# A four-step 16-bit minimum for the key distances, and a quarter of the dense units masked through ScalarE and TensorE

## The chip, the cores and the metric

One core of a Trainium2 chip runs the whole program. The metric is the device time of one execution in microseconds (us). Engines are named as in the profile: PE (TensorE matmul), PEld (its weight loads), DVE (VectorE), ACT (ScalarE), POOL (GpSimd), SP (SyncE, which only issues DMAs).

## The reference, cut to what matters

32 independent items (batches) go through three stages. A convolutional tokenizer makes 128 channels by 64 positions. A linear-attention mixer works on rows of 64. Then a product-key feed-forward with 8 heads follows, of which the core is:

```
sim = einsum(q, pk_keys)                  # two lists of 64 scores per row and head
scores, idx = top_k(sim, 16)              # the best 16 of each list
score = scores[0][:, None] + scores[1][None, :]      # 256 pairs
final_scores, pk_idx = top_k(score, 16)   # the best 16 pairs -> rows of a 4096-row table per head
weights = softmax(final_scores)
kv = sum over the 16 chosen rows of weights * table[row]
```

The table has 4096 rows per head, each of 128 numbers (64 of key, 64 of value); a small causal attention per head follows on kv.

## The kernel before, in words

Each batch is cut into stages: tokenizer (T), mixer (M), `route` (R, top 16 and row numbers of heads 0 to 3), `second` (S, the same for heads 4 to 7), `dense` (D), `group` (G, sums of gathered rows) and `head` (H, the attention).

Heads 0 to 4 are **gathered**: POOL issues 16 indirect DMAs per head (L1090), each fetching 128 rows of 512 bytes into one of three buffers `got`. These are 5 x 16 x 32 = 2560 gathers. A gather of group n waits for the PE sum of group n-3 (`s_summed`, L1381), because there are three buffers; group 0 of a batch waits for the row numbers that `route` writes (L1930), group 4 for those of `second` (L2127). PE sums a group at hop `a{g}`, which waits until the group has landed.

Heads 5 to 7 are **dense**: no rows are fetched, but all 4096 table rows of the head, kept in SBUF (`tab`, 2 MB a head, three heads), are multiplied by weights of which all but 16 are zero. A head has 16 units of 256 rows, a batch has 48, the kernel 1536. A unit u is: PE `p{u}` (`pair_scores`: two matmuls L1337 for the scores, two matmuls L1339 for the distances, 128x128 bf16 each, into one of two PSUM banks); ACT `x{u}` (L1642, exp of the 256 scores); DVE `w{u}` (L2203, which keeps the weight where the distance is under 15.5); PE `v{u}` (`table_sum`, L1359, two fp32 products, four records).

The **distance** of each of the 64 keys of a list from the chosen ones is made in `second`, hops `o{i}{k}`, for the 6 lists of the dense heads: four DVE additions give 64 x 16 differences in fp16 (L2150, 256 elements each), and two reductions over the last axis of 16 take the smallest absolute value (L2155, 512 elements in, 32 out each). Both lists' distances are added in the matmuls L1339.

The **order** of all work is written out by hand-made tables: `AT` gives every hop of every stage a due time in units of a millionth of a batch, `OWN` replaces it for some batches, `plan()` sorts all hops of all batches, and each engine issues its instructions in that one order. Nothing is chosen at run time: an engine waits at the front of its queue. Before the change the sorted order has, on DVE ahead of the first row numbers of batch 0, the hops `r0` to `row_d` of `second` and `n0` of batch 2's tokenizer.

Of the kernel before, what the change touches and what calls it, by code (L numbers as in the profile page):

```python
# [19 lines left out]
F16 = mybir.dt.float16  # L20
ALU = mybir.AluOpType
# [18 lines left out]
DENSE = (5, 6, 7)  # L40
ND = len(DENSE)
NG = HEADS - ND
# [3 lines left out]
UNITS = ND * TILES  # L46
# [16 lines left out]
QUARTER = 4  # L63
PARTS = 4
# [74 lines left out]
def tower(nc, x, consts, pairs, w0, w1, w2, w3, cvec, mw1, mw2, mw3, mb1, mb2, mb3, stack, mix, bw, ba, bg, vec64,  # L139
          wo_attn, gn, wqpk, keys, wq, table, wo_ffn, parts, out):  # L140
    ctx = ExitStack()
    with ctx:
# [135 lines left out]
        tab = sb("tab", [P, ND, CHUNKS, P])  # L278
        d_w = sb("d_w", [P, 2, 2, P])
        kvd = sb("kvd", [P, ND, P])  # L280
# [81 lines left out]
        s_stack = [sem(f"s_stack{i}") for i in range(2)]  # L362
        s_pairs = sem("s_pairs")
        s_d_exp = sem("s_d_exp")
        s_d_w = sem("s_d_w")
        s_d_sum = sem("s_d_sum")
# [30 lines left out]
        block = ctx.enter_context(nc.Block())  # L397

# [31 lines left out]
        for n, k in enumerate(("xd", "proj", "lora", "ss", "tri", "p0", "t0", "p1", "t1", "p2", "t2", "p3", "t3", "p4", "t4",  # L430
# [8 lines left out]
        R2 = {k: n for n, k in enumerate(each_list + [  # L439
            "idx", "cand", "keys", "fin8", "codes", "code", "rep_f0", "rep_f1", "rep_f2", "rep_f3", "fin16_0", "fin16_1", "fin16_2", "fin16_3", "fidx",  # L440
            "place", "early", "shift", "pick_e0", "row_e0", "pick_l0", "row_l0",
            "row_d", "row_t", "rep_d", "row_h", "code0", "chosen", "code1", "depth", "code2", "code3"]
            + [f"{k}{i}{j}" for i in range(ND) for j in range(2) for k in ("miss", "near", "half", "dist")]
            + ["fsum", "frec", "weight", "w_t", "shifted"], 1)}
        NROUTE, NSECOND = len(R), len(R2)

# [19 lines left out]
        def group_hops(u):  # L466

            last = u == UNITS - 1
            return ([(f"v{u - 1}", 0.9)] if u else []) + ([(f"k{u - 1}", 0.4)] if u and u % TILES == 0 else []) + (
                [(f"p{u + 1}", 1.2)] if not last else []) + ([("s2", 0.1)] if u == TILES else []) + (  # L470
                [(f"x{u}", 0.6), (f"w{u}", 0.8)]) + ([(f"v{u}", 0.9), (f"k{u}", 0.4)] if last else [])
# [12 lines left out]
        def choose_hops(pieces):  # L484
            return ([("r0", 1.2), ("r1", 1.2), ("r2", 2.2), ("r3", 1.2), ("r4", 1.2), ("cands", 0.5), ("keys", 0.5), ("fin8", 0.8), ("codes", 1.2),
                     ("finx", 0.7), ("repf", 1.0), ("fin16", 0.8), ("fidx", 0.7), ("early", 0.5), ("shift", 0.4), ("e", 0.0)]
                    + [x for k in range(pieces) for x in ((f"e{k}", 1.0), (f"l{k}", 1.2), (f"lr{k}", 1.1))])

        ROUTE_HOPS = choose_hops(2) + [("row_t", 0.2), ("fsum", 0.2), ("rows", 0.2), ("frec", 0.1), ("weight", 0.1), ("w_next", 0.8)]
        SECOND_HOPS = (choose_hops(1) + [("row_d", 0.2), ("rd0", 0.3), ("row_t", 0.1), ("rd1", 0.3), ("row_h", 0.2), ("chosen", 0.2), ("rows", 0.2), ("depth", 1.2), ("codes2", 0.5)]  # L490
                       + [(f"o{i}{k}", t) for i in range(ND) for k, t in ((0, 1.2), (1, 1.2), (2, 1.2), (3, 1.2))]
                       + [("fsum", 0.2), ("lnf", 0.5), ("frec", 0.1), ("weight", 0.1), ("w2", 0.8), ("sh", 0.4)])
        DENSE_HOPS = ([("dt", 1.4), ("dc", 0.8), ("dr", 0.5), ("dm", 0.5), ("dl", 0.5), ("sw", 0.1), ("s0", 0.1), ("s1", 0.1), ("p0", 1.2)]
                      + [x for u in range(UNITS) for x in group_hops(u)])

        STEP = 1000000

        AT = (
            (
# [431 lines left out]
        def plan():  # L931

            order = []
            for b in range(BATCH):
                for stage, hops in enumerate(HOPS):
                    if stage == b == 0:
                        hops = FIRST_CONV + hops[len(FIRST_CONV):]
# [33 lines left out]
        def each(count, unit):  # L971

            def program(b):
                for u in range(count):
                    yield from unit(b, u)
# [1307 lines left out]
```

## Time and profile before

| what | value |
|---|---|
| time, median of 3 runs | 3446.4 us (3445.68 to 3448.38) |
| profiled execution, span from its first to its last instruction | 3442.5 us |
| what lies around that span, against the median | 3.9 us |
| PE, DVE, ACT, POOL busy | 90%, 83%, 61%, 72% of the span |
| first gather starts, last gather starts | 153.8 us, 3406.1 us |
| mean granted TensorE clock | 0.984 |

The profiled execution has no time of its own beside its span; the difference to the median is taken as what lies around it. "Busy" leaves out the time in which an engine issues a DMA, so POOL at 72% has to be read with its idle time: the view of waits says what ended each idle stretch, and "issue" there means that nothing was waited for. PE's busy time counts the modelled ends of pipelined matmuls: a 128x128 bf16 product is shown with 0.22 us, while the next one starts 0.05 to 0.06 us later.

### The profile page before, as it was taken

What the parts mean: (1) busy time and instruction counts of PE and PEld (TensorE: products, weight loads), DVE (VectorE), ACT (ScalarE), POOL (GpSimd) and SP (SyncE); (2) the same over time, 40 slices, a digit from 0 to 9 for tenths busy, and PEclk for the clock granted to TensorE, in tenths of its full rate; (3) what the DMA queues carried; (4) which work ended last, traced back from release to release, by engine and by line L of the source; (5) the groups of instructions that cost most, each with busy time, mean ns of one, the idle gap of its engine ahead of it and who ended that gap; (6) DMA issues with size and microseconds to landing.
All of it is one profiled execution on the core that took longest, in us unless ns stands there. A gap on an engine that the chain in (4) does not pass through costs nothing.

```text
span 3442.5 us, 79362 instructions
## 1 busy us (share of the span) xinstructions
PE 3091.9 (90%) x25850; PEld 2384.2 (69%) x25850; DVE 2856.3 (83%) x14978; ACT 2103.0 (61%) x5921; POOL 2469.3 (72%) x2571
## 2 busy tenths in 40 slices
PE   9999999889999989999999999998999999888777
PEld 6776667677667666666767766776766676766666
DVE  3688888988888988888898888888888888888762
ACT  5456666666666666666566666666666666665333
POOL 0177777777777777777777777777777777777774
PEclk9999999999999999999999999999999999999888
DMA  7022222222222222222222222222222222222221
GB/s 159 11 74 71 72 66 69 74 74 76 69 74 61 74 75 75 74 69 69 65 75 73 75 68 75 61 74 74 74 75 69 71 64 75 75 75 68 66 77 41
DMA packets 307373, 245.84 MB, mean 71 GB/s; under 512 B 246600, under 2 KB 259440, under 8 KB 306832
## 3 DMA queue, kind: packets, MB, share of 16 engines
q0 software_dynamic: 81920, 167.94, 17.8%
q1 hardware_dynamic: 225040, 72.83, 9.1%
q8 instruction: 206, 3.38, 0.4%
q14 instruction: 207, 1.70, 0.2%
HBM read 230.06 MB, written 10.49 MB: 70 GB/s over the span
## 4 chain that ended last, share of the span: by engine, by line
POOL 53%; issue 19%; PE 16%; DVE 9%; ACT 4%; DMA 0%; POOLq 0%; SPq 0%; DVEq 0%; ACTq 0%
POOL got L1090 53%; PE bank L1359 3%; PE bank L1180 3%; DVE d_w L2203 1%; PE bank L1198 1%; PE bank L1109 1%; PE bank L1337 1%; PE bank L1339 1%; PE bank L1381 1%; DVE top L1938 1%; PE bank L1126 1%; DVE dist L2155 0%; DVE topi L1942 0%; DVE pick L2150 0%; ACT L1432 0%
## 5 line engine op out<-in xcount | busy, mean ns | idle before, releaser
L1090 POOL DMA_INDIRECT got<-in_table,rows x2560 | 2466.4, 963 | 936.9 <-issue 777.7
L1359 PE MATMUL bank<-d_w,tab 128*128 128x128 f32 x6144 | 1055.9, 295 | 136.5 <-DVE d_w L2203 128.9
L1359 PEld LDWEIGHTS bank<-d_w,tab 128*128 128x128 f32 x6144 | 827.4, 195 | 325.3 <-DVE d_w L2203 214.5
L2203 DVE SCALAR_TENSOR_TENSOR d_w<-bank,d_w 128x256 f32<-128x256 f32 x1536 | 633.6, 414 | 168.3 <-ACT d_w L1642 159.0
L1642 ACT ACTIVATE d_w<-bank 128x256 f32<-128x256 f32 x1536 | 579.6, 380 | 276.6 <-PE bank L1339 258.5
L1337 PE MATMUL bank<-stacked,stack_sel 128*128 128x128 bf16 x3072 | 428.5, 222 | 12.3 <-issue 11.5
L1339 PE MATMUL bank<-d_dist,sel 128*128 128x128 bf16 x3072 | 428.7, 222 | 0.0
L1180 PE MATMUL bank<-h,conv_w 128*128 128x512 f32 (+2 forms) x1024 | 330.6, 469 | 0.5 <-DVE h L1789 0.4
L1337 PEld LDWEIGHTS bank<-stacked,stack_sel 128*128 128x128 bf16 x3072 | 306.8, 100 | 35.0 <-issue 15.2
L2155 DVE TENSOR_REDUCE dist<-pick 128x32 f32<-128x512 f16 x384 | 261.7, 682 | 6.6
L1180 PEld LDWEIGHTS bank<-h,conv_w 128*128 128x128 f32 x1024 | 171.8, 189 | 119.7 <-issue 109.2
L1339 PEld LDWEIGHTS bank<-d_dist,sel 128*128 128x128 bf16 x3072 | 240.7, 99 | 0.0
L1381 PE MATMUL bank<-got,spread_w 128*32 128x128 f32 x5120 | 176.6, 277 | 52.6 <-DMA got<-in_table,rows 28.5
L1518 ACT ACTIVATE square<-bank,cbias 128x512 f32<-128x512 f32 (+2 forms) x96 | 48.7, 508 | 250.2 <-PE bank L1180 250.1
L1381 PEld LDWEIGHTS bank<-got,spread_w 128*32 128x32 f32 x5120 | 135.6, 110 | 90.9 <-issue 79.3
L2150 DVE TENSOR_TENSOR pick<-misses,key_codes 128x256 f16<-128x256 f16 x768 | 190.3, 282 | 0.0
L1432 ACT ACT_TABLE_LOAD x128 | 164.2, 1283 | 3.0 <-PEq L2251 0.7
L1163 PE MATMUL bank<-shared 64*128 64x512 f32 x248 | 138.3, 637 | 7.4 <-DVE normed L1749 7.2
L1198 PE MATMUL bank<-mlp,normed 128*128 128x512 f32 x256 | 118.4, 605 | 24.6 <-ACT normed L1462 24.6
L1167 PE MATMUL bank<-square,cst 128*128 128x512 f32 x248 | 133.8, 621 | 7.2 <-ACT square L1442 7.2
L1451 ACT ACTIVATE h<-normed,chan 128x512 f32<-128x512 f32 x124 | 100.4, 810 | 61.1 <-DVE normed L1770 61.1
L1683 ACT ACTIVATE prob_t<-bank 128x128 f32<-128x128 f32 x256 | 70.8, 277 | 95.9 <-PE bank L1419 95.5
(329 smaller groups left out, 6391.6 us busy)
## 6 DMA issues: line engine op xcount, KB each, us to landing
got<-in_table,rows POOLq DMA_INDIRECT x2560, 2.5
stacked<-parts SPq DMA_DIRECT2D x576, 64.0 KB
parts<-d_parts SPq DMA_DIRECT2D x32, 288.0 KB
stacked<-parts SPq DMA_DIRECT2D x576, 16.0 KB
tab<-in_table SPq DMA_DIRECT2D x24, 256.0 KB, 8.3
got<-in_pairs SPq DMA_DIRECT2D x1, 2048.0 KB, 9.7
shared<-in_x SPq DMA_DIRECT2D x32, 50.0 KB
mlp<-in_mw SPq DMA_DIRECT2D x1, 1024.0 KB, 8.9
```

What stands on the lines that cost most here:

```text
L1090: pool.indirect_dma_start(got[:, n % NGB, k, :], None, table, bass.IndirectOffsetOnAxis(ap=rows[:, b % 2, g * TOPK + k:g * TOPK + k + 1], ...
L1180: last = mm(conv_bank[:, 0:LEN[n - 1]], conv_w[n][:, k, :], rhs, start=k == 0, stop=k == taps - 1)
L1198: last = mm(conv_bank[:, :], z1[:, k, :], mlp2[:, k, :], start=k == 0, stop=k == MC - 1)
L1337: mm(ps[:, x * P:(x + 1) * P], stack_sel[:, x, :], stacked[:, n % 2, tile, :], start=x == 0, stop=False)
L1339: last = mm(ps[:, (2 + x) * P:(3 + x) * P], sel[:, c + x, :], d_dist[:, b % 2, i, :], start=False, stop=x == 1)
L1359: last = mm(acc_bank[:, i * P:(i + 1) * P], tab[:, i, 2 * tile + x, :], d_w[:, u % 2, x, :], start=tile == x == 0, stop=tile == TILES - 1 ...
L1381: last = mm(kv_rows_ps[t * BLOCK:(t + 1) * BLOCK, :], spread_w[:, at:at + BLOCK], got[:, n % NGB, k, :], start=i == 0, stop=i == QUARTER - 1)
L1432: exp_and_ln = lambda: nc.scalar.preload_act_table_set("natural_log_exp_and_others")
L1642: a(d_w[:, u % 2, :, :].rearrange("p k t -> p (k t)"), pair_bank[u % 2][:, 0:2 * P], ACT.Exp).then_inc(s_d_exp, 1)
L2150: return tt(apart[:, a:a + quarter_keys, :], misses[:, upper, i, k, :].unsqueeze(1).broadcast_to(full), key_codes[:, a - upper * half:a - ...
L2155: return v.tensor_reduce(dist[:, i, k, at:at + half], apart[:, at:at + half, :], AX.X, ALU.min, apply_absolute_value=True)
L2203: stt(both, pair_bank[u % 2][:, 2 * P:4 * P], TOPK - 0.5, both, ALU.is_lt, ALU.mult).then_inc(s_d_w, 1)
```

## The change

It has four parts.

1. **Tree of minima.** The 64 x 16 differences of a list go through two in-place minima of halves (16 to 8 to 4 per key) on their bits read as 16-bit unsigned integers, and one reduction of 4. Two lists alternate between two halves of the scratch, so that each step of one list stands behind additions of the next.
2. **Gated units.** Units 1, 5, 9 and 13 of every dense head (12 of 48 a batch) have no DVE mask. ACT computes relu(distance - 15) (`g{u}`), PE adds the scores and -16384 times that value to the bank (`a{u}`: the two score matmuls, which move there from `p{u}`, and one 128x256 bf16 matmul), ACT takes the exp, PE sums.
3. **Streamed table.** Two dense tables stay in SBUF. That of head 5 comes through a ring of three buffers of 512 KB, four refills a batch on SP's queue, each after the units that used its buffer: 2 MB a batch, 128 DMAs, some 64 MB in all. Structures for batches with four dense heads are there (`KIND`, `nd_of`), but `KIND` is "N" for all 32 batches: every batch keeps 5 gathered and 3 dense heads.
4. **Order.** `AT` has other due times throughout, and `OWN` is left only for the tokenizer and mixer of batch 0, the groups of batch 1 and `second` of batch 31. Sorted, ahead of the first row numbers of batch 0 there now stand only `r0` to `codes` of `second` and no `n0` of batch 2; `finx`, `repf`, `fin16`, `fidx`, `early`, `shift`, `e0`, `l0`, `lr0` and `row_d` come behind. In the steady part the hop `a0` stands ahead of `v45`, and behind `v44`; before, `w44`, for which `v44` waits, stood on DVE behind `r2`, `r3` and `r4` of `route`; now these stand behind `w44`.

```
-DENSE = (5, 6, 7)
+KIND = "NNNNNNNNNNNNNNNNNNNNNNNNNNNNNNNN"
+FOUR = "E"
+RESIDENT = 2
+GATED = (1, 5, 9, 13)
+FAR = 16384.0
...
-        tab = sb("tab", [P, ND, CHUNKS, P])
+        tab = sb("tab", [P, RESIDENT, CHUNKS, P])
+        ring = sb("ring", [P, RING, CHUNKS // QUARTER, P])
...
+            def refill(n):
+                b = max(x for x in range(BATCH) if Q0[x] <= n)
+                h, q = ng_of(b) + (n - Q0[b]) // QUARTER, n % QUARTER
+                sp.dma_start(ring[:, n % RING, :, :].rearrange("p c d -> p (c d)"), stream[h - HALF, q, :, :]).then_inc(s_ring[n % RING], 16)
...
+                            if u % TILES == TILES - 1:
+                                sp.wait_ge(s_d_sum, D0[b] + u // TILES + 1)
+                            else:
+                                sp.wait_ge(s_ring_used, n - n // QUARTER + 1)
+                            refill(n + RING)
...
+                    if gated(u):
+                        yield f"a{u}"
+                        pe.wait_ge(s_d_gate, gates(b, u) + 1)
+                        scores(b, u, False)
+                        mm(pair_bank[u % 2][:, 0:2 * P], far[:, :], gate_by[:, :, :].rearrange("p k t -> p (k t)"), start=False, stop=True).then_inc(s_d_gated, 1)
...
+                    if gated(u):
+                        yield f"g{u}"
+                        act.wait_ge(s_pairs, D0[b] * TILES + u + 1)
+                        act.wait_ge(s_d_gated, gates(b, u))
+                        a(gate_by[:, :, :].rearrange("p k t -> p (k t)"), pair_bank[u % 2][:, 2 * P:4 * P], ACT.Relu, bias=eps[:, 3:4]).then_inc(s_d_gate, 1)
...
-                            return v.tensor_reduce(dist[:, i, k, at:at + half], apart[:, at:at + half, :], AX.X, ALU.min, apply_absolute_value=True)
...
+                def fewer(n, left):
+                    x = bits[n % 2]
+                    return tt(x[:, :, 0:left], x[:, :, 0:left], x[:, :, left:2 * left], ALU.min)
+
+                def nearest_rank(n):
+                    return v.tensor_reduce(dist[:, n // 2, n % 2, :], apart[n % 2][:, :, 0:TOPK // 4], AX.X, ALU.min, apply_absolute_value=True)
...
+                    apart_from(n, 0)
+                    apart_from(n, 1)
+                    if n:
+                        own(f"eight{n - 1}")
+                        inc(fewer(n - 1, TOPK // 4))
+                    yield f"o{n // 2}{n % 2 * 2 + 1}"
+                    apart_from(n, 2)
+                    inc(apart_from(n, 3))
+                    if n:
+                        own(f"four{n - 1}")
+                        inc(nearest_rank(n - 1))
+                    own(f"apart{n}")
+                    inc(fewer(n, TOPK // 2))
...
-                for u in range(UNITS):
+                for u in (u for u in range(units(b)) if not gated(u)):
```

## Rows read from the trace of the kernel before

**Rows 1.** Waits of POOL: who was waited for, total us, times, longest.

```profile
POOL got L1090 <- issue: 777.7, 2551, 0.4
POOL got L1090 <- DVE rows L1930: 150.9, 4, 150.0
POOL got L1090 <- PE bank L1381: 8.3, 5, 6.2
```

**Rows 2.** The page's groups of L1090 and L1359: busy, mean ns, idle.

```profile
L1090 POOL DMA_INDIRECT got<-in_table,rows x2560 | 2466.4, 963 | 936.9 <-issue 777.7
L1359 PE MATMUL bank<-d_w,tab 128*128 128x128 f32 x6144 | 1055.9, 295 | 136.5 <-DVE d_w L2203 128.9
```

**Rows 3.** All instructions of L1090: ns min/median/max, first and last start us.

```profile
L1090 POOL DMA_INDIRECT got<-in_table,rows x2560: 938/944/2226, 153.8 to 3406.1; - x197
```

**Rows 4.** Timeline, batch 6: row numbers; first gather; sum and gather; last sum.

```profile
759.91 0.22 DVE L1930 TENSOR_TENSOR rows<-row_t,cst 128x64 uint32<-128x64 f32 x1
...
764.64 0.94 POOL L1090 DMA_INDIRECT got<-in_table,rows  x1 [0.30 <-issue]
...
820.15 0.28 PE L1337 MATMUL bank<-stacked,stack_sel 128*128 128x128 bf16 x2
820.27 0.28 PE L1339 MATMUL bank<-d_dist,sel 128*128 128x128 bf16 x2
820.47 1.08 PE L1381 MATMUL bank<-got,spread_w 128*32 128x128 f32 x32
...
825.59 0.94 POOL L1090 DMA_INDIRECT got<-in_table,rows  x1 [0.30 <-issue]
...
867.30 1.08 PE L1381 MATMUL bank<-got,spread_w 128*32 128x128 f32 x32 [0.69 <-DMA got<-in_table,rows]
```

**Rows 5.** Stretch 400 to 800: busy us of PE, PEld, DVE, ACT, POOL; clock; DMA.

```profile
400.00:800.00 400.00, 361.85 (x3090) 276.99 (x3090) 351.14 (x1855) 256.95 (x726) 304.06 (x315) 1.00 0.27 72
```

**Rows 6.** Groups by shape on DVE and ACT: busy, mean ns of one, idle.

```profile
L2203 DVE SCALAR_TENSOR_TENSOR d_w<-bank,d_w 128x256 f32<-128x256 f32 x1536 | 633.6, 414 | 168.3 <-ACT d_w L1642 159.0
L2155 DVE TENSOR_REDUCE dist<-pick 128x32 f32<-128x512 f16 x384 | 261.7, 682 | 6.6
L2150 DVE TENSOR_TENSOR pick<-misses,key_codes 128x256 f16<-128x256 f16 x768 | 190.3, 282 | 0.0
L1890 DVE TENSOR_TENSOR inv<-bank,inv 128x256 f32<-128x256 f32 x160 | 66.8, 418 | 42.7 <-PE bank L1268 42.0
L1642 ACT ACTIVATE d_w<-bank 128x256 f32<-128x256 f32 x1536 | 579.6, 380 | 276.6 <-PE bank L1339 258.5 <-issue 9.0
```

**Rows 7.** Timeline of DVE, 142 to 150, ahead of the first row numbers.

```profile
142.14 0.08 DVE L1994 MATCH_VALUE_LOAD finp<-fin,cand 128x8 f32 x1
...
145.38 0.56 DVE L2003 MAX8 fin<-cand 128x8 f32<-128x54 f32 x4
...
147.36 0.32 DVE L2046 TENSOR_TENSOR pick<-early,place 128x160 f32<-128x160 f32 x1
...
149.91 0.48 DVE L2046 TENSOR_TENSOR pick<-early,place 128x320 f32<-128x320 f32 x1
```

**Rows 8.** Timeline, 3256 to 3268: PE, then POOL.

```profile
3263.26 1.22 PE L1359 MATMUL bank<-d_w,tab 128*128 128x128 f32 x4 [5.44 <-DVE d_w L2203]
...
3264.84 1.94 PE L1381 MATMUL bank<-got,spread_w 128*32 128x128 f32 x32
...
3267.03 1.00 POOL L1090 DMA_INDIRECT got<-in_table,rows  x1 [6.21 <-PE bank L1381]
```

**Rows 9.** Timeline, two slow gathers and what ran on DVE at their start.

```profile
562.96 0.27 DVE L1867 TENSOR_TENSOR right<-lin_a,dec_dn 64x128 f32<-64x128 f32 x1
...
563.09 1.37 POOL L1090 DMA_INDIRECT got<-in_table,rows  x1 [0.30 <-issue]
...
587.04 0.69 DVE L2150 TENSOR_TENSOR pick<-misses,key_codes 128x256 f16<-128x256 f16 x3
...
587.27 1.07 POOL L1090 DMA_INDIRECT got<-in_table,rows  x1 [0.30 <-issue]
```

More of the change, by code:

```diff
@@ L397, in tower, with nd_of, ng_of, single @@
         block = ctx.enter_context(nc.Block())
+        def nd_of(b):
+            return 4 if KIND[b] in FOUR else 3
+        def ng_of(b):
+            return HEADS - nd_of(b)
+        def single(b):
+            return ng_of(b) > HALF
+        def before(count):
+            return [sum(count(x) for x in range(b)) for b in range(BATCH + 1)]
+        def streamed(b):
+            return nd_of(b) - RESIDENT
+        G0, D0, S0_, Q0 = before(ng_of), before(nd_of), before(single), before(lambda b: streamed(b) * QUARTER)
+        LAST_SUM = G0[BATCH] - 1
+        def units(b):
+            return nd_of(b) * TILES
+        def gated(u):
+            return u % TILES in GATED
+        def masked(b, u):
+            return D0[b] * (TILES - len(GATED)) + sum(not gated(x) for x in range(u))
+        def gates(b, u):
+            return D0[b] * len(GATED) + sum(gated(x) for x in range(u))
+        def last_batch(b, has):
+            return next((x for x in range(b - 1, -1, -1) if has(x)), None)
         def head_at(b, p):
@@ L973, in program @@
             def program(b):
-                for u in range(count):
+                for u in range(count(b)):
                     yield from unit(b, u)
@@ L1422, in head @@
                 mm(y_ps, prob_t[:, :], vw[:, :], start=True, stop=True).then_inc(s_y, 1)
-            pipeline(pe, tokenizer, mixer, nothing, nothing, dense, each(NG, group), each(HEADS, head))
+            pipeline(pe, tokenizer, mixer, nothing, nothing, dense, each(ng_of, group), each(lambda b: HEADS, head))
         @block.scalar
@@ L1683, in head @@
                 a(prob_t[:, :], prob_ps, ACT.Copy).then_inc(s_prob_t, 1)
-            pipeline(act, tokenizer, mixer, route, second, dense, each(NG, group), each(HEADS, head))
+            pipeline(act, tokenizer, mixer, route, second, dense, each(ng_of, group), each(lambda b: HEADS, head))
         @block.vector
@@ L2238, in head @@
                 stt(res_o[:, :] if p == HEADS - 1 else res[:, b % 3, :], y_ps, erec[:, :], res[:, b % 3, :], ALU.mult, ALU.add).then_inc(s_added, 1)
-            pipeline(vec, tokenizer, mixer, route, second, dense, each(NG, group), each(HEADS, head))
+            pipeline(vec, tokenizer, mixer, route, second, dense, each(ng_of, group), each(lambda b: HEADS, head))
 _OUT = (BATCH, C, D)
```

432 lines of the change are left out of this document (252 added, 180 removed), and 468 rows, old and new, of tables (AT, OWN).

## The prediction, on record before the result was known

> **What bounds the kernel now.** First the waits of POOL, because POOL is busy 72% on the page and looks idle for the rest. In [rows 1] it waited 150.0 us for the first row numbers, 8.3 us in all for PE, and otherwise only for "issue", 777.7 us in 2551 pieces. So from 153.8 us on POOL never rests: 2560 gathers take 2466.4 us [rows 2] and 777.7 us of issue between them, 3244 us. From the first gather's start to the last one's [rows 3] are 3406.1 - 153.8 = 3252.3 us, 1.271 us a gather, 101.6 us a batch of 80. The time is therefore
>
> 153.8 (until the first gather) + 3252.3 (gathers) + 36.4 (from the last gather's start to the end of the 3442.5 us span) = 3442.5 us, and 3.9 us around it to the median 3446.4.
>
> Then the timeline of one batch, to see how far everything else is from that bound. In [rows 4] the row numbers of batch 6 are written at 759.91 + 0.22 and used at 764.64: 4.5 us early. The sum of its group 0 ends at 821.55, the gather that needs its buffer starts at 825.59: 4.0 us early. And PE stands 0.69 us idle until the batch's last group lands, at 867.30. So PE, the in-order engine that all others follow, is held by POOL once a batch, but by under 1 us: it is nearly as slow as POOL. [rows 5] says why: in a steady stretch of 400 us PE is busy 361.85, DVE 351.14, ACT 256.95; in a batch of 101.6 us that is 91.9, 89.2 and 65.3 us. What the change takes from DVE is not on the path; what it may do is shift the three terms above, or slow PE until POOL starts to wait.
>
> **Part 1, the tree.** Per list, before: 4 additions of 0.282 and 2 reductions of 0.682 [rows 6], 2.49 us. After: the same 4 additions; a minimum of 512 elements; one of 256; a reduction of 256. L2150 does 256 elements of 16 bits in 0.282 and L1890 256 of 32 bits in 0.418, so 16 bits go two at a time in the additions. Like them, the minima cost 0.418 (512) and 0.282 (256); as slow as the 16-bit reduction L2155, 0.682 and 0.418. The reduction of 256 takes about 0.418, as it takes elements one at a time. Sum 2.25 us, or 2.65 at the other end: six lists a batch, -1.5 us of DVE a batch, or +0.9. I take -1.5, since the same instruction kind with fp16 shows it. Hidden either way behind POOL.
>
> But DVE and POOL do touch. The median gather lasts 944 ns and the mean 963 [rows 2, 3]: 0.019 x 2560 = 49 us are lost. In [rows 9] the gather at 563.09 took 1.37 where additions with both inputs in SBUF ran back to back over its start, 0.43 more; the one at 587.27 took 1.07 beside three L2150, 0.13 more. The tree adds 192 x (0.418 + 0.282) = 134 us of such instructions; the reductions that go have one input and the masks that go read PSUM. Bounds: 0, if only chance overlaps count and phases improve; 0.13 / 0.69 x 134 = 25 us at the rate of the second slow gather, which was picked for being slow. DVE has some 800 us of two-input work in SBUF for the 49 us (my sum over its groups; L2150 alone is 190), 0.06 us per us: 134 x 0.06 = **+8 us**, which I take. As the new order moves every overlap, the old 49 us may also come out 15 lower or higher.
>
> The Trainium skill, "SBUF — State Buffer", section "Who interferes with whom", says that a VectorE instruction with two SBUF inputs contends with a GpSimd instruction that reads SBUF, but infers that descriptor generation needs only the write interface, by which this term would be 0 and the sum 8 us less. The 1.37 us gather beside such additions speaks for contention, so the trace weighs more here.
>
> **Part 2, the gated units**, 12 a batch. DVE loses 12 x 0.414 = 5.0 us a batch. ACT gains 12 relus of 256 from PSUM, 0.380 each by L1642 [rows 6]: +4.6 us, to 69.9 of 101.6, room enough. PE: the two score products move and don't grow; added is one bf16 product over 256 columns. Two such over 128 columns start 820.27 - 820.15 = 0.12 us before the next pair [rows 4]: +0.12 us, 1.4 us a batch; with its weight load and a bubble not hidden at most twice that, 2.9. Waits: `a{u}` waits for the relu, and behind it on PE stand `v{u}` and everything else in order, sums and heads too; the following exp waits for `a{u}`. In exchange `v{u}` no longer waits for DVE behind ACT. PE idled 128.9 us for such masks [rows 2], 4.0 a batch, of which a quarter, 1.0 us, belongs to the units that lose them. The relu can run while PE waits for the mask of the unit before (`p{u}` is issued a unit ahead), so I take a wash: PE +0.4 us a batch net, between -2 (DVE's relief shortens the other waits) and +4. Against it stands the 0.69 us of slack per batch. Just covered.
>
> **Part 3, the stream.** 64 MB beside 246 MB; the DMA engines are busy 0.27 in [rows 5], so about 0.07 more. POOL does not wait for landings. PE waits for the ring only at every fourth unit, three quarters (12 units, some 20 us) after the refill was issued. Cost 0; if a landing of group 4 comes 3 us late, the 4.0 to 4.5 us margins of [rows 4] cover it, and without them it would be 3 x 31 = 93 us, far off. SP holds the refills in order with the spreading of the parts; the one for the third dense head stands behind a refill of 512 KB, but is needed 15 units later.
>
> **Part 4, the order**, sorted from the tables.
> - *Start.* Eight pieces of `second` and one of batch 2's tokenizer no longer stand on DVE ahead of the first row numbers. Between 147.36 and 149.91 [rows 7] DVE did nothing else: 2.55 us. Between 142.14 and 145.38 it did them beside four replacements of `route` (0.74) and the statistics of the mixer (0.35): 3.24 - 1.09 = 2.15 us. DVE has no wait there, so the first gather moves by **-4.7 us**, to 149.1; between -8 and 0, as the other moves may add a wait. Behind it, the row numbers have a later hurdle only in batch 1, 4 us wide before; due times put them 0.06 batch, 6 us, earlier against the last sum.
> - *The one real stall.* POOL waited 6.21 us at 3267.03 for the sum at 3264.84, which stood behind an L1359 product that waited 5.44 us for DVE [rows 8]: DVE did `r2` to `r4` of the last batch first. Now these stand behind that mask. **-6.2 us**, at worst 0.
> - *Steady.* Row numbers come about 6 us earlier and the sum of group 0 about 2 us earlier against the sum that PE and POOL meet at, by the due times. No gain, more margin.
> - *End.* Behind the last gather stand the same 22 units and five heads; five of the units are gated. Where one is alone, exp + mask (0.38 + 0.41) becomes relu + scores and gate (0.3 with hand-overs) + exp: +0.3 to +0.45 each. **+2 us**, between 0 and +4.
>
> **Sum.** -4.7 - 6.2 + 8 + 2 = -0.9 us on 3446.4: **3445.5 us**. No change.
>
> **The rivals.** About what can be told from no change is 0.2%, 6.9 us: 3439.5 to 3453.3.
> - *A. No change* (the sum above, 3445.5; with the uncertain terms at half their width 3440 to 3453). For it: gathers and their count stay as they are. Against: three terms of 5 to 8 us must cancel. Chance 0.38.
> - *B. The two savings without the contention*: 3446.4 - 4.7 - 6.2 + 0 + 2 = 3437.5; with favourable overlaps 3433. For it: of the additions L2150 most stand beside gathers of 0.94 us, so that 16-bit operands may hold POOL less than my mean rate; the phases of DVE and POOL are locked each batch, so 49 us is partly bad luck. Chance 0.31.
> - *C. PE becomes the bound.* Place: `a{u}` and the far product, in order on PE. If PE's batch takes d us more than now, the 0.69 us of slack [rows 4] is gone from d = 0.7, the 4.0 us of buffer margin then lasts 4 / (d - 0.7) batches, and after that POOL waits 31 x (d - 0.7). With the full 1.4 us and the waits no shorter: 31 x 0.7 - 4 = 18 us, 3445.5 + 18 = 3463; at 2.9 us, 64 us. For it: PE busy 91.9 of 101.6 and held so little at the meeting point. Against: DVE gives up 6.5 us of 89.2, and 4.0 us a batch of PE's idle time is waiting for DVE. Chance 0.31, with it all of "slower".
> - *D. The minima on unsigned integers don't go two at a time.* DVE +0.9 us a batch, and two-input time 192 x 1.1 = 211 us, +13 us of contention instead of 8: 3451; part of A and C, not counted apart.
>
> The Trainium skill, "VectorE: DVE Perf Modes", section "Mode 2×_1P — pack two bf16 into one 32-bit read", asks for 16-bit types and step 1, whatever the type; by it D does not happen. No row here shows an unsigned 16-bit instruction.
>
> Range 3434 to 3468: it leaves out the heavy half of C and the best corner of B. Faster by over 0.2% 0.31, within 0.38, slower 0.31. The likeliest case's own range is 3440 to 3453.
>
> **What would show it.** First gather near 149 us. POOL's waits for PE near 2 us, not 8; if C, they are tens of us at group starts, and PE's wait for the landing of group 4 is gone. L1090's mean 966 ns (A) or 961 (B). New DVE minima 0.42 and 0.28. L2203's count 1152, and 384 relus of 0.38. The last gather's start to the end 38 us. Wrong altogether: if POOL's mean gather changes by over 10 ns, or it waits for DMA landings or rows.

## The result, and the profile after

The changed kernel takes 3777.6 us (median of 4 runs, 3766.9 to 3786.0) against 3446.0 us before (3445.4 to 3448.4): ratio 1.0958, 95% interval 1.0934 to 1.0982. The forecast was 3445.5 us with a range of 3434 to 3468. It was wrong, by 332 us, on the side to which it gave a chance of 0.31 and no more than 64 us.

First the waits of POOL after (who was waited for, total us, times, longest), beside [rows 1]:

```profile
POOL got L838 <- issue: 759.4, 2465, 1.9
POOL got L838 <- DVE rows L1716: 256.0, 32, 144.3
POOL got L838 <- PE bank L1153: 215.6, 63, 10.6
```

The waits for PE went from 8.3 us in 5 pieces to 215.6 in 63 (about two a batch), those for row numbers from 150.9 to 256.0. The first gather is as early as forecast (148.1 us, next row), but POOL no longer sets the time: it stands still before the groups of every batch. All gathers of the kernel after, with min/median/max ns and the first and last start, beside [rows 3]; then groups by shape, beside [rows 2, 6]:

```profile
L838 POOL DMA_INDIRECT got<-in_table,rows x2560: 938/944/2217, 148.1 to 3743.6; - x197
```

```profile
L838 POOL DMA_INDIRECT got<-in_table,rows x2560 | 2509.8, 980 | 1231.0 <-issue 759.4 <-DVE rows L1716 256.0 <-PE bank L1153 215.6
L1129 PE MATMUL bank<-d_w,tab 128*128 128x128 f32 x4096 | 750.7, 311 | 176.4 <-DVE d_w L2021 165.2 <-ACT d_w L1424 7.8 <-issue 0.3
L1424 ACT ACTIVATE d_w<-bank 128x256 f32<-128x256 f32 x1536 | 555.4, 380 | 457.8 <-PE bank L1099 313.7 <-PE bank L1113 129.9 <-issue 9.5
L1418 ACT ACTIVATE gate_by<-bank,eps 128x256 bf16<-128x256 f32 x384 | 180.2, 469 | 226.4 <-PE bank L1099 219.9 <-issue 4.5
L1953 DVE TENSOR_TENSOR pick<-pick 128x512 uint16<-128x512 uint16 x192 | 80.0, 416 | 1.1
L1953 DVE TENSOR_TENSOR pick<-pick 128x256 uint16<-128x256 uint16 x192 | 54.4, 283 | 0.0
L1956 DVE TENSOR_REDUCE dist<-pick 128x64 f32<-128x256 f16 x192 | 79.0, 411 | 0.0
```

The mean gather went from 963 to 980 ns, though the median is still 944. L1129 is the old L1359, and its product of the tables in SBUF takes 311 ns in place of 295, on the same data. Why, the windows say (start:end, length, busy us of PE, PEld, DVE, ACT, POOL, granted clock, DMA share, GB/s). First 400 to 800, beside [rows 5], then three neighbouring stretches inside it:

```profile
400.00:800.00 400.00, 360.96 (x2880) 277.89 (x2878) 301.00 (x1698) 250.28 (x715) 281.92 (x287) 0.93 0.32 85
430.00:437.20 7.20, 4.86 (x23) 2.80 (x22) 6.93 (x60) 3.87 (x9) 5.44 (x6) 1.00 0.62 161
437.40:451.00 13.60, 12.97 (x91) 11.22 (x89) 9.60 (x68) 4.54 (x14) 10.01 (x10) 0.50 0.42 120
451.10:461.00 9.90, 9.58 (x108) 7.61 (x104) 6.55 (x49) 7.03 (x24) 6.96 (x8) 1.00 0.33 99
```

PE is busy as long as before (360.96 of 400 us against 361.85), with 7% fewer instructions. The granted clock is 0.93 in place of 1.00, and from 437.4 to 451.0 it is 0.50: TensorE runs at 1.2 GHz instead of 2.4. "Busy" hides it, since 91 slow products in 13.6 us fill PE as well as 108 in the next 9.9. Product by product the factor is two: in this trace two bf16 products in a row on line L1099 start 56 ns apart at 2.4 GHz and 107 at 1.2, two fp32 ones on L1129 112 and 214 (medians). What PE did just before it fell (timeline of PE; start, us, and in brackets the idle time before):

```profile
434.10 0.71 PE L1129 MATMUL bank<-d_w,tab 128*128 128x128 f32 x4 [0.27 <-DVE d_w L2021]
434.65 0.27 PE L1159 MATMUL bank<-cst,kv_rows 128*128 128x128 f32 x1
436.99 0.38 PE L1129 MATMUL bank<-d_w,tab 128*128 128x128 f32 x1 [2.07 <-DVE d_w L2021]
```

DVE at that time, the last pair of the search and the mask:

```profile
436.33 0.08 DVE L1734 MATCH_VALUE_LOAD dist<-top,sims 128x8 f32 x1
436.40 0.20 DVE L1734 MATCH_REPLACE8 dist<-top,sims 128x64 f32<-128x64 f32 x1
436.52 0.41 DVE L2021 SCALAR_TENSOR_TENSOR d_w<-bank,d_w 128x256 f32<-128x256 f32 x1
```

PE stood for 2.07 us until the mask of unit 47 (436.52 to 436.93), which stood on DVE behind eight match-and-replace pairs of the top-16 search (from 434.97). The other regular stand-still is at unit 19, whose exp stands on ACT behind two tanh and the table loads ahead of and behind them (ACT, then PE):

```profile
475.38 1.28 ACT L1326 ACT_TABLE_LOAD   x1
476.68 0.36 ACT L1326 ACTIVATE sig_wa<-bank,v64h 64x128 f32<-64x128 f32 x1
476.94 0.35 ACT L1327 ACTIVATE sig_wa<-bank,v64h 64x128 f32<-64x128 f32 x1
...
477.42 1.28 ACT L1205 ACT_TABLE_LOAD   x1
478.71 0.38 ACT L1424 ACTIVATE d_w<-bank 128x256 f32<-128x256 f32 x1
```

```profile
479.61 0.71 PE L1129 MATMUL bank<-d_w,tab 128*128 128x128 f32 x4 [2.09 <-DVE d_w L2021]
```

Between 400 and 3300 us there are 53 stand-stills of over 1.5 us, and at 49 of them the clock fell between their beginning and 4 us behind their end, mostly behind it, as here (436.99 and 437.37). In the kernel before there are 5 such stand-stills in that stretch, and PE was at 1.2 GHz for 61 us of it, against 480 after. Not every fall is accounted for: 45 of the 65 after belong to one of the 53, and most of the others (16) come at a wait of 0.94 us, ahead of the transpose of gathered sums. A wait of middle length seldom did it by itself: the kernel before has 60 of 1.0 to 1.5 us in the same stretch and 7 falls in all.

**The loss in one sum.** From the first gather of batch 3 to that of batch 28, divided by 25, a batch takes 112.88 us after and 101.42 before, 11.46 more. PE's busy time at 1.2 GHz is 17.42 us a batch (1.07 before); half of that would not be there at full clock, so the clock takes (17.42 - 1.07) / 2 = **8.18 us**. PE's idle time went from 9.06 to 11.51, **+2.45**. The rest of its busy time went from 91.82 to 92.65, **+0.83**. All runs below can be split up in this way; the table's column "at 1.2 GHz" is all of the batch's time at that clock, of which PE is busy nine tenths or more (17.42 of 18.59 after). That half of the busy time is the right share is seen in three runs with the same products on PE: e5, e13 and e10 have 1.90, 10.76 and 17.28 us of it a batch, and the rest of their busy time is 91.9, 91.4 and 91.6.

| run | ratio to before (95%) | us | a batch | PE idle | at 1.2 GHz | mean gather, ns |
|---|---|---|---|---|---|---|
| before | 1 | 3446.0 | 101.42 | 9.06 | 1.09 | 963 |
| after | 1.0958 (1.0934 to 1.0982) | 3777.6 | 112.88 | 11.51 | 18.59 | 980 |
| e1 no gated units | 1.1035 (1.0992 to 1.1078) | 3797.5 | 113.72 | 13.82 | 18.02 | 972 |
| e2 old order | 1.1336 (1.1309 to 1.1363) | 3903.6 | 116.94 | 16.49 | 12.42 | 975 |
| e3 neither | 1.0094 (1.0074 to 1.0114) | 3479.5 | 103.01 | 10.19 | 3.28 | 982 |
| e4 two places filled | 1.0798 (1.0772 to 1.0824) | 3716.2 | 110.44 | 10.43 | 11.06 | 979 |
| e5 ring alone | 1.0010 (1.0000 to 1.0019) | 3450.3 | 102.01 | 9.18 | 1.91 | 963 |
| e6 tree alone | 1.0095 (1.0078 to 1.0111) | 3479.9 | 103.24 | 10.02 | 4.37 | 985 |
| e7 three moves | 1.0908 (1.0890 to 1.0926) | 3760.8 | 112.06 | 11.37 | 16.79 | 981 |
| e8 two moves | 1.0938 (1.0919 to 1.0956) | 3773.1 | 112.92 | 11.73 | 18.71 | 979 |
| e9 three places filled | 1.0685 (1.0656 to 1.0713) | 3691.8 | 110.36 | 9.05 | 7.53 | 983 |
| e10 new order, ring | 1.1141 (1.1115 to 1.1166) | 3843.4 | 115.24 | 15.01 | 18.57 | 958 |
| e11 first minimum twice | 1.0149 (1.0130 to 1.0169) | 3502.5 | 102.97 | 9.71 | 3.41 | 982 |
| e12 start moved | 1.0002 (0.9990 to 1.0014) | 3451.6 | 101.72 | 9.33 | 0.82 | 965 |
| e13 one stand-still | 1.0537 (1.0521 to 1.0553) | 3627.5 | 107.35 | 10.53 | 10.82 | 961 |
| e14 four places filled | 1.0608 (1.0588 to 1.0627) | 3654.6 | 108.57 | 8.69 | 2.05 | 979 |
| e15 series broken up | 1.0104 (1.0089 to 1.0120) | 3480.2 | 102.81 | 9.73 | 3.69 | 979 |
| e16 before, series broken | 0.9978 (0.9967 to 0.9988) | 3436.7 | 101.47 | 8.94 | 1.09 | 953 |
| e17 minima on fp16 | 1.0119 (1.0103 to 1.0136) | 3491.4 | 102.49 | 9.37 | 3.41 | 976 |
| e18 e16 and start moved | 0.9966 (0.9954 to 0.9978) | 3442.0 | 101.49 | 8.96 | 1.09 | 956 |

Each ratio is to runs of the kernel before on the same chip (medians 3445.0 to 3453.9), so the ratio decides where two runs are near each other. The last four columns are of the one execution that was profiled. e14 is the median of two executions.

### The profile page after: what moved, and what is told of

It reads as the page before. It is cut to its first block, busy times and chain, and to the rows that moved or that the text cites. A ratio compares the mean times of both kernels' runs of the same rounds, so it can differ in the third digit from the quotient of the medians.

```text
span 3779.7 us, 80765 instructions
## 1 busy us (share of the span) xinstructions
PE 3363.1 (89%) x26234; PEld 2594.2 (69%) x26234; DVE 2695.3 (71%) x14788; ACT 2245.3 (59%) x6305; POOL 2512.7 (66%) x2571
## 4 chain that ended last, share of the span: by engine, by line
PE 65%; DVE 17%; ACT 11%; issue 4%; POOL 2%; DMA 0%; SPq 0%; POOLq 0%; ACTq 0%; DVEq 0%
PE bank L1129 18%; PE bank L928 8%; PE bank L1084 4%; PE bank L1153 4%; PE bank L1099 4%; PE bank L915 3%; DVE d_w L2021 3%; PE bank L911 3%; ACT d_w L1424 2%; POOL got L838 2%; PE bank L1188 2%; DVE topi L1744 2%; PE bank L1015 2%; DVE sims L1734 2%; PE bank L857 1%
## 5 line engine op out<-in xcount | busy, mean ns | idle before, releaser
L838 POOL DMA_INDIRECT got<-in_table,rows x2560 | 2509.8, 980 | 1231.0 <-issue 759.4
L1129 PE MATMUL bank<-d_w,tab 128*128 128x128 f32 x4096 | 750.7, 311 | 176.4 <-DVE d_w L2021 165.2
L1129 PEld LDWEIGHTS bank<-d_w,tab 128*128 128x128 f32 x4096 | 596.6, 209 | 309.0 <-DVE d_w L2021 230.9
L2021 DVE SCALAR_TENSOR_TENSOR d_w<-bank,d_w 128x256 f32<-128x256 f32 x1152 | 480.8, 420 | 450.7 <-ACT d_w L1424 446.2
L1099 PE MATMUL bank<-d_dist,sel 128*128 128x128 bf16 x3072 | 453.4, 235 | 0.0
L1129 PE MATMUL bank<-d_w,ring 128*128 128x128 f32 x2048 | 400.0, 324 | 26.6 <-DVE d_w L2021 9.4
L1129 PEld LDWEIGHTS bank<-d_w,ring 128*128 128x128 f32 x2048 | 311.8, 217 | 80.3 <-DVE d_w L2021 41.1
L1418 ACT ACTIVATE gate_by<-bank,eps 128x256 bf16<-128x256 f32 x384 | 180.2, 469 | 226.4 <-PE bank L1099 219.9
L1099 PEld LDWEIGHTS bank<-d_dist,sel 128*128 128x128 bf16 x3072 | 278.9, 108 | 22.8 <-issue 16.6
L2046 DVE CUSTOM_DVE_ANT_0 neg<-bank,cst 128x128 f32<-128x128 f32 x256 | 74.0, 289 | 131.2 <-PE bank L1189 129.8
L1676 DVE TENSOR_TENSOR inv<-bank,inv 128x256 f32<-128x256 f32 x160 | 67.5, 422 | 126.9 <-PE bank L1016 126.8
L1440 ACT ACTIVATE kv_rows<-bank 128x128 f32<-128x128 f32 x160 | 44.3, 277 | 177.9 <-PE bank L1153 177.9
## 6 DMA issues: line engine op xcount, KB each, us to landing
tab<-in_table SPq DMA_DIRECT2D x16, 256.0 KB, 8.9
```

Source lines behind the costliest of these rows:

```text
L838: pool.indirect_dma_start(got[:, n % NGB, k, :], None, table, bass.IndirectOffsetOnAxis(ap=rows[:, b % 2, g * TOPK + k:g * TOPK + k + 1], ...
L1099: last = mm(ps[:, (2 + x) * P:(3 + x) * P], sel[:, c + x, :], d_dist[:, b % 2, i, :], start=gated(u) and x == 0, stop=x == 1)
L1129: last = mm(acc_bank[:, i * P:(i + 1) * P], of, d_w[:, u % 2, x, :], start=tile == x == 0, stop=tile == TILES - 1 and x == 1)
L1418: a(gate_by[:, :, :].rearrange("p k t -> p (k t)"), pair_bank[u % 2][:, 2 * P:4 * P], ACT.Relu, bias=eps[:, 3:4]).then_inc(s_d_gate, 1)
L2021: stt(both, pair_bank[u % 2][:, 2 * P:4 * P], TOPK - 0.5, both, ALU.is_lt, ALU.mult).then_inc(s_d_w, 1)
```

## The experiments

### Which part it is (e1, e2, e3, e5, e6, e10)

```
# e1: after, every unit masked on DVE; exp due where the relu was, mask where the exp was
-GATED = (1, 5, 9, 13)
+GATED = ()
# e2: after, with AT and OWN of before (relu and add due with the old exp, exp with the old mask)
# e3: both edits. e5: e3 with the two reductions a list of before. e6: e3 with three tables in SBUF, no ring
# e10: e1 with the two reductions a list of before
# (e6, e11 and e13 also leave out the buffers' room for a fourth dense head, which no batch has)
```

e1: 

> The kernel after, with no gated units: all 48 units of a batch are masked on DVE again (exp where the relu stood, mask where the exp stood); tree, ring and the new order stay. If the gated units' longer chain through PE makes the loss (theory G), the time falls to 3440 to 3460 us. If the new order makes it (theory O), PE still stands about 2 us twice a batch, once behind an activation-table load and once behind a piece of the top-16 search, the granted clock stays near 0.92, and the time stays above 3650. If both are needed, it lies between, 3500 to 3600.

e2: 

> The kernel after with the due times of the kernel before (relu and add due where the exp was, exp where the mask was); tree, gated units and ring stay. Theory O: 3440 to 3480 us, at a granted clock of 0.98. Theory G: above 3600, and PE waits for the gated units. If the new order was made to carry the gated units, this is slower than the kernel after.

e3: 

> The kernel after with neither gated units nor new due times: the kernel before with the tree and the ring alone, in the same order of work. Both theories: 3435 to 3460 us. If the ring or the tree costs something by itself (theory R), it is over 3480.

Both simple theories fell. Without the gated units the new order is no better (1.1035), and with the old order the gated units are worse (1.1336). Only without both is the time back, at 1.0094. So each of the two is enough by itself, and the new order loses less with the gated units than without. The waits of ACT in e2 and e3 show how the gated units do it in the old order (L1195 is the product with `far`, L1181 the distance product):

```profile
ACT d_w L1506 <- PE bank L1195: 692.2, 347, 7.4
...
ACT d_w L1506 <- PE bank L1181: 160.1, 202, 7.4
```

```profile
ACT d_w L1506 <- PE bank L1181: 281.5, 381, 7.0
```

The exp of an ungated unit needs only `p{u}`, which PE issues a unit ahead, so ACT runs ahead of PE. That of a gated unit needs `a{u}`, which stands in PE's own queue just ahead of the sums: in 347 of 384 cases ACT stood still for it, 2.0 us each, and all that ACT owed to others waited too. POOL's waits for row numbers went to 412.2 us in that run, PE's idle time from 10.19 to 16.49 us a batch.

e10: 

> Of the change the new order and the ring, which cost nothing by itself; distances and masks as in the kernel before. If the new order alone loses the time: 3740 to 3790 us, clock near 0.92. If the order needs the tree to lose it (its distances take DVE otherwise), under 3600.

It lost even more than expected, 3843.4 us, with no tree and no gated unit: idle 15.01 us a batch, 18.57 at 1.2 GHz, mean gather 958 ns. The order by itself makes the stand-stills: between 400 and 3300 us there are 75 of over 1.8 us.

e5: 

> Order, gated units and distances as in the kernel before; only the streamed ring is new. Where the 30 us of the run without gated units in the old order come from: theory 'the ring's traffic': the mean gather is near 980 ns (before 963) and the time about 3480 us; theory 'the tree's two-input minima hold POOL': the mean gather stays at 963 and the time within 3440 to 3455 us, but for a wait of PE for the stacked weights behind the ring on the DMA queue.

e6: 

> Order, gated units and the three tables in SBUF as in the kernel before; only the tree of 16-bit minima is new. By the traffic theory: mean gather 963 ns or a little over, 3440 to 3455 us. By the contention theory: mean gather near 980 ns, 3475 to 3485 us. Minima of 512 and 256 elements at 0.42 and 0.28 us.

The ring costs nothing (1.0010). The 0.95% are the tree's alone. The gathers in e5, e6 and e3:

```profile
L919 POOL DMA_INDIRECT got<-in_table,rows x2560 | 2465.8, 963 | 945.5 <-issue 775.8 <-DVE rows L1797 159.2 <-PE bank L1234 10.6
```

```profile
L910 POOL DMA_INDIRECT got<-in_table,rows x2560 | 2521.2, 985 | 931.0 <-issue 777.9 <-DVE rows L1787 151.0 <-PE bank L1225 2.1
```

```profile
L920 POOL DMA_INDIRECT got<-in_table,rows x2560 | 2515.1, 982 | 930.7 <-issue 773.4 <-DVE rows L1798 150.9 <-PE bank L1235 6.4
```

With the tree POOL is the bound still (it waits 2.1 and 6.4 us for PE), and 80 gathers of 19 to 22 ns more are 1.5 to 1.8 us a batch, which is what the batch became longer by (103.01 and 103.24 against 101.42).

### Is it the clock, and what makes it fall (e4, e9, e14, e13)

```
# e4: unit 20's scores and distances made six times, the transpose of group 0's sums seven times
-                for x in range(2):
+                for again in range(6 if u == 20 else 1):
+                    if again: scores(b, u, False)
+                    for x in range(2): ...
# e9: nine and fifteen times, and 16 products into unit 0's bank ahead of its wait for the stacked weights
# e14: e9, and the distances of unit 1 six times
# e13: e5 (old order) with, ahead of the mask of unit 19,
+                        for at in range(4):
+                            v.tensor_reduce(spare[:, at, :], key_codes[:, :, :], AX.X, ALU.min)
```

e4: 

> The kernel after, with PE kept at work just ahead of its two 2.07 us waits of each batch: the scores and distances of unit 20 are made six times in place of once, and one transpose of gathered sums seven times in place of once; the same data, the same waits. If the lost time is mostly the fallen clock (theory C), the granted clock returns towards 0.98 and the time falls to 3540 to 3600 us, though PE has more work; if the waits alone cost it, the time stays at 3770 or rises, and the clock with its stretches at 1.2 GHz stays.

It went in theory C's direction and not as far as expected: 3716 us in place of 3540 to 3600. The extra work left 0.97 and 1.4 us of the two waits, and the wait for the stacked weights stayed.

e9: 

> The kernel after with PE kept at work at three places of every batch: unit 20's scores and distances made nine times, the first transpose of gathered sums fifteen times, and sixteen products into the bank of unit 0 ahead of the wait for the stacked weights; nothing else waits less. Theory C (PE standing still for 2 us makes the clock fall, and the clock is two thirds of the loss): time at half clock falls from 18.4 us a batch to under 4, and the time to 3550 to 3610 us. If the clock falls by something else, it stays near 0.92 and the time is 3770 or more, since PE has some 4 us a batch more to do.

Again it stopped half way: 7.53 us a batch at 1.2 GHz and 3691.8 us. Now a wait of 1.1 to 1.6 us stood behind the distances of unit 1 in most batches, and 16 of the 30 falls between 400 and 3300 us came at one or within 4 us of its end.

e14: 

> The run with three places filled, and a fourth: the distances of unit 1 made six times, ahead of the wait that was 1.2 to 1.4 us in it. Theory C: half clock under 3 us a batch (7.4 with three places), and in spite of 0.6 us more work the time falls from 3692 to 3630 to 3660. If the clock doesn't answer to this gap, 3700 or more.

3654.6 us, as expected, with 2.05 us a batch at 1.2 GHz (columns as above, stretch 400 to 3100; ahead of it the same stretch of the kernel after, with nothing filled):

```profile
400.00:3100.00 2700.00, 2424.32 (x19031) 1862.27 (x19030) 1998.66 (x11030) 1670.02 (x4717) 1877.85 (x1915) 0.92 0.32 83
```

```profile
400.00:3100.00 2700.00, 2482.72 (x21608) 1916.15 (x21607) 2082.06 (x11477) 1736.60 (x4910) 1948.35 (x1989) 0.99 0.34 86
```

PE does 6.2 us a batch more work than after, all of it useless, and the kernel is 123 us faster. This is theory C's best evidence in the new order: work in place of standing still gives the clock back, from 0.92 to 0.99.

e13: 

> Old order, no gated units, no tree (the kernel at 3450 us), with four reductions of 512 elements into a spare buffer on DVE ahead of the mask of unit 19: the mask comes up to 2.7 us late, once a batch. Theory C (standing still makes the clock fall): some 12 us behind it PE runs at half clock in most batches, 3 to 8 us a batch, and the time is 3560 to 3650, about twice what the stand-still explains. Otherwise the clock stays at 0.98 and only the stand-still beyond the slack is paid, 1.5 to 2 us a batch: 3490 to 3515.

3627.5 us, in the range of theory C and 110 us above the other's. One stand-still and what followed (PE; DVE; then windows ahead of it, of the slow stretch and behind that):

```profile
1004.36 0.27 PE L1181 MATMUL bank<-d_dist,sel 128*128 128x128 bf16 x2
1006.61 0.71 PE L1211 MATMUL bank<-d_w,tab 128*128 128x128 f32 x4 [1.97 <-DVE d_w L2089]
```

```profile
1003.77 2.45 DVE L2086 TENSOR_REDUCE spare<-key_codes 128x32 f16<-128x512 f16 x4
1006.14 0.41 DVE L2089 SCALAR_TENSOR_TENSOR d_w<-bank,d_w 128x256 f32<-128x256 f32 x1
```

```profile
998.00:1006.60 8.60, 5.95 (x76) 4.81 (x75) 7.68 (x20) 5.96 (x19) 6.67 (x7) 1.00 0.70 169
1008.60:1018.70 10.10, 10.10 (x37) 6.65 (x37) 6.40 (x37) 5.86 (x16) 6.68 (x7) 0.50 0.18 46
1018.90:1029.00 10.10, 9.81 (x97) 7.51 (x97) 9.14 (x34) 6.37 (x15) 7.96 (x8) 1.00 0.19 49
```

The clock fell at 1008.51, 1.9 us behind the end of the stand-still and not the 12 us that the expectation named (a misreading of the record's time base). In the slow 10.1 us PE issued 37 products, in the next 97. Not each stand-still does it: of 27 over 1.5 us between 400 and 3300, 24 have a fall between their beginning and 4 us behind their end, and the 54 waits of 1.2 to 1.4 us that this kernel also has, nearly as the kernel before has them, have one. Against e5 the batch is 5.34 us longer: (10.76 - 1.90) / 2 = 4.43 clock, 1.35 idle time, the rest 0.44 less. Beside each microsecond of added idle time stand some three that the clock cost.

### Can the stand-stills be moved away (e7, e8)

```
# e7: three due times; e8 without the third
+        MOVED = {(4, 'x19'): 2977131, (4, 'w47'): 3609064, (4, 'dl'): 2537923}
```

e7: 

> The kernel after with three hops earlier in its order: the exp of unit 19 ahead of the tanh of the mixer (and its table load), the mask of unit 47 ahead of a piece of the top-16 search, and the last subtraction of the parts two units earlier, so that the stacked weights of the next batch land before they are waited for. If the clock falls because PE stands still for some 2 us twice a batch (theory C), the clock is near 0.98 and the batch takes what its work and its other waits take, 101.5 to 104.5 us: 3480 to 3570. If the clock falls for another reason (theory L: the work itself, fp32 and bf16 mixed otherwise), the clock stays near 0.92 and the time above 3700.

e8: 

> As the run with three moves, without the move of the subtraction: PE still waits 0.7 to 2.3 us for the stacked weights of a new batch. Between the kernel after and the run with three moves; near the latter (under 3580) if the two waits for masks carried the loss, near 3700 if the wait for the landing is enough to let the clock fall.

Both failed: 3760.8 and 3773.1 us. Stand-stills of over 1.5 us between 400 and 3300 us are 50 in e7 and 48 in e8, against 53 after: they had moved and not gone. So clock and time came out as theory L said, without deciding against theory C, since PE went on standing still; e13 and e14 decide that. In e7 the 2.07 us ahead of unit 47 are gone, and PE reaches `p0` of the next batch that much earlier (SP's DMA issues, then PE):

```profile
875.28 0.39 SPq L757 DMA_DIRECT2D parts<-d_parts  x1
877.90 0.31 SPq L769 DMA_DIRECT2D stacked<-parts  x1
```

```profile
881.25 0.28 PE L1094 MATMUL bank<-stacked,stack_sel 128*128 128x128 bf16 x2
886.38 0.37 PE L1094 MATMUL bank<-stacked,stack_sel 128*128 128x128 bf16 x2 [3.11 <-issue]
```

There it waits 3.11 us. The profile says "issue"; what the kernel waits for at this place is the landing of the stacked weights, whose chain begins only with `dt` at 869.5 (transposes, copies, subtractions, a store, 12 loads: 17 us until 886.4). That the wait for the mask had hidden this one is inferred from their order. No single move pays here.

### Why the gathers are longer (e11, e15, e17, e16)

Timeline of e6: DVE in a stretch of the tree, then POOL:

```profile
795.88 0.41 DVE L2024 TENSOR_TENSOR pick<-pick 128x512 uint16<-128x512 uint16 x1
796.21 0.48 DVE L2019 TENSOR_TENSOR pick<-misses,key_codes 128x256 f16<-128x256 f16 x2
796.61 0.28 DVE L2024 TENSOR_TENSOR pick<-pick 128x256 uint16<-128x256 uint16 x1
796.82 0.48 DVE L2019 TENSOR_TENSOR pick<-misses,key_codes 128x256 f16<-128x256 f16 x2
797.22 0.41 DVE L2027 TENSOR_REDUCE dist<-pick 128x64 f32<-128x256 f16 x1
```

```profile
795.95 2.18 POOL L910 DMA_INDIRECT got<-in_table,rows  x1 [0.30 <-issue]
```

A gather that began 0.07 us behind the first minimum took 2.18 us in place of 0.94: 1.24 more, about the 1.34 us of the unbroken series of two-input instructions (795.88 to 797.22). In e6 24 gathers take over 1.8 us, in before 2. The series of six occurs 94 times, one gather begins in each, and these lose 44.7 us; in before 52 gathers begin in a series of three additions and lose 2.9 us.

```
# e11: e3 with the first minimum also into a spare buffer
+                    tt(spare[:, :, :], bits[n % 2][:, :, 0:TOPK // 2], bits[n % 2][:, :, TOPK // 2:TOPK], ALU.min)
# e15: e3; order a0 a1 | reduce keys 32-63 of list n-2 | min 4, a2 a3 | reduce keys 0-31 of n-1 | min 8
# e17: e3 with x = apart[n % 2] (fp16) in place of bits[n % 2] in the minima; it leaves out the absolute value
# e16: before, mixer and pair masks
+                inc(ts(kfac...))        # behind left_k, was behind kk; and right_b ahead of k2
+                inc(cp(bonus...))       # ahead of the three offs, was behind them
```

e11: 

> The kernel with tree and ring in the old order (3479.5 us, mean gather 982 ns), with the first minimum of each list made twice, the first time into a spare buffer: 192 more instructions of 512 elements, 79 us of DVE. If two-input minima on DVE hold POOL's gathers (theory H), the mean gather rises by a third to two thirds of what the tree added, to 990 to 998 ns, and the time by 20 to 40 us. If the 19 ns come from elsewhere (theory S: shifted phases between DVE and POOL), it stays at 980 to 986.

The mean gather stayed at 982 ns with 79 us more of such work; the series are as many and only longer. Inside these series the gathers lost more (51.5 us in 95 gathers, in e3 40.7 in 94, counted over 0.944 us each), and elsewhere less. The time rose to 1.0149 (3502.5) all the same; its profiled execution (a span of 3485.5 us, as in e3) doesn't show where, so that stays open. The amount of two-input work is not the measure of the mean.

e15: 

> Tree and ring in the old order (3479.5 us, mean gather 982 ns), with the same additions and minima, but the reduction of each list in two halves, one between the second addition and the second minimum, one ahead of the first minimum: no more than three two-input instructions stand in a row where there were six. Theory K (a gather that starts inside a long unbroken series waits for its end): mean gather 963 to 970 ns, 3445 to 3460 us. If the sum of two-input work decides, 980 ns and 3475 us or more.

Theory K fell as stated: 979 ns, 1.0104. The series of three that begin with a minimum (743 ns) now catch 124 gathers and cost them some 35 us, 280 ns each, where series of three additions (682 ns, before) cost 2.9.

e17: 

> Tree and ring in the old order (3479.5 us, mean gather 982 ns), with the minima of halves taken on fp16 numbers with their signs in place of 16-bit integers (so the distances are not the smallest absolute values; same counts, sizes and places). If unsigned integers are what holds the gathers, the mean gather falls to 965 or less and the time to 3450; if any minimum of two 16-bit halves does, both stay, 978 to 986 ns and 3475 to 3490 us.

976 ns, 1.0119: the integer type is not it. What is left is that series with minima of two plain 16-bit halves hold POOL, and additions alone whose one operand is broadcast hardly do. No run separates the operation from the form of its operands, or from the moment in the series at which the gathers begin.

e16: 

> The kernel before with two one-input instructions set in the middle of series of two-input ones: kfac behind four of the eight products of the mixer, the bonus copy ahead of the three blocks of offs. Theory K: the 12.4 + 4.7 us that gathers lose inside these two series fall to a half or less, mean gather 957 to 960 ns, time 3436 to 3442. If the series don't matter: 3446 to 3450.

In the kernel before, series of products in fp32 did cost gathers: seven in a row in the mixer 12.4 us, six at the pair masks 4.7. With one-input instructions set in their middle the mean gather is 953 ns and the time 3436.7 us, ratio 0.9978 (0.9967 to 0.9988): **faster than both kernels**. The gathers gained 26 us, the kernel 8: POOL's waits for PE rose from 8.3 to 29.8 us, as PE is the next bound.

### The start (e12, e18)

```
# before; in batch 0, the hops finx to row_t of second are due just behind rows of route
+                        at = [max(t, rows) if k in moved else t for k, t in enumerate(at)]
```

e12: 

> The kernel before with one thing of the new order: in batch 0 the hops finx to row_t of second stand behind the first row numbers instead of ahead of them. The first gather starts 4 us earlier, near 149.7 us, and all else follows: 3442 us, against 3446 to 3448. If the work put off comes back at the first wait for group 4's row numbers, no gain.

e18: 

> The run with the two series broken up (3436.7 us), and the piece of second moved behind the first row numbers. As the moved piece alone gave nothing (the first gather came 2.2 us earlier in its profile, of 4 expected), 3433 to 3437.

e12: the first gather started at 151.6 us in place of 153.8, not 149.7, and no gain can be measured (1.0002). e18 is at 0.9966 (0.9954 to 0.9978), not to be told from e16.

## Why the prediction was wrong, by its steps

The prediction let PE's batch grow by 0.4 us, at most by 4; it grew by 11.46. These steps made the difference:

- **"Part 2 ... Waits ... I take a wash: PE +0.4 us a batch net ... Just covered": failed.** It counted what PE itself waits for at a gated unit, and not that ACT, which had run ahead of PE, is tied to PE's place in its queue. In the old order this costs 1.1336 / 1.0094 (e2 against e3), 13.9 us a batch: 6.3 idle, 4.2 clock, 3.5 other busy time of PE. In the new order the gated units did no such harm: 1.0958 with them, 1.1035 without (e1).
- **"Part 4 ... Steady ... No gain, more margin": failed.** It looked at the two places where PE and POOL meet, by due times, and not at what stands on ACT and DVE ahead of each unit's exp and mask. The new order alone costs 11% (e10), so this step by itself is enough for the miss: the exp of unit 19 behind a table load, the mask of unit 47 behind the search, `dt` to `p0` too short.
- **The clock was in no term.** [rows 5] showed 1.00, and it was taken as given. It is 8.18 of the 11.46 us a batch. e13 and e14 show both directions. The Trainium skill, "TensorE: Matmul & The Clock Gate", section "HAM oscillation — how this bites in real kernels", describes a kernel whose recurring waits for DMA, of 3 to 5 us, throttle TensorE again and again. The traces here agree that recurring waits do it, and show it at waits of 2 us, in a queue that is 90% busy.
- **Rival C was right that PE becomes the bound, and wrong on where and by how much.** It put the loss at `a{u}` and the far product; without any gated unit the new order loses no less (e1). Its formula, 31 x (d - 0.7) - 4, gives 330 us with d = 11.46, and 332 were lost, but that only says that every batch grew alike: this d is the growth of the whole batch, measured afterwards. Its own d ended at 2.9 us because only the added product was counted. That part was no more than 0.83 us of work a batch, against 1.4.
- **Part 1, the instructions: right** (0.416, 0.283 and 0.411 against 0.418, 0.282 and 0.418), so rival D is out. **The contention, +8 us with 25 as its end: mis-sized.** Alone it is 0.95%, 33 us, at 19 to 22 ns a gather. The rate was an average over two-input work that hardly contends, and the "additions" that it read in [rows 9] at 563.09 are the seven products of the mixer, the series that e16 broke up. The direction was right, and against the inference in the Trainium skill, "SBUF — State Buffer", section "Who interferes with whom", that descriptor generation stays clear of such an instruction: the gather of 2.18 us shows otherwise, and the measurement decides. A gather here also reads its row numbers from SBUF (`rows`), and no run separates that read from the rest of its work.
- **Part 3, the ring, 0: right** (e5). The relu, which unlike the exp reads a bias, takes 0.469 us, not 0.380: mis-sized; what that is worth no run shows.
- **The start, -4.7: right** in the kernel after (148.1 against 153.8, -5.7); by itself (e12) it gave nothing that can be measured. **The end** took 36.2 us, not 38, where 36.4 stood before: mis-sized. **The stall of 6.21 us** no longer had a meaning, as POOL waited everywhere. The prediction's own signs of being wrong altogether came: the mean gather changed by 17 ns, and POOL waited for row numbers in every batch.

## What to carry to other kernels

Where TensorE is 90% busy and the granted clock is 1.00, write the clock into the sum as a term of its own: ask of each edit whether it makes PE stand still in one piece where it did not before. Here 1.35 us of such idle time a batch cost 5.34. In queues issued in a fixed order, moving one operation to another engine ties that engine to the other's place; list what each engine had run ahead by, not only what it is busy with. Where gathers bound a kernel, look at what VectorE runs at their start: two one-input instructions, each in the middle of a long series of two-input ones, were worth 8 us here.

## What was not expected of the hardware

- A stand-still of 1.97 us once a batch, put into a kernel at a clock of 0.98, cost 5.3 us a batch; filling four waits with useless products made another kernel 123 us faster.
- A gather of 0.94 us lasted 2.18 us beside a series with 16-bit minima on VectorE. Doubling those minima made no gather longer on average; fp16 or unsigned integers made no difference.
- ScalarE's relu from PSUM to bf16 with a bias took 0.469 us for 128x256, its exp to fp32 without one 0.380.
